# A two-layer graph attention kernel: which queue stores the packed mask, and the order of four partition quarters

## Chip, cores and metric

The kernel runs on one core of one Trainium2 chip. The metric is the device time of one execution in microseconds (us). Three executions of the kernel before took 2398.2, 2375.98 and 2375.66 us; the median is 2375.98 us.

## What is computed

`x` is 8192 nodes by 128 features (float32), `adj` an 8192 by 8192 matrix of int32 zeros and ones. Two layers follow each other; cut to what matters, each is:

```
h = maximum(layernorm(x), 0)
Wh = h @ W + b
e = leaky_relu((Wh @ a1)[:, None] + (Wh @ a2)[None, :], 0.2)
attention = softmax(where(adj > 0, e, -9e15), axis=1)
x = x + attention @ Wh
```

Both layers read the same 256 MB of adjacency. The result is `x` after the second layer.

## The kernel before, in words

The 8192 rows are cut into 64 tiles of 128 rows. Since leaky_relu of a sum has two slopes, exp of it splits into two products; a tile therefore needs only two 0/1 masks per edge (edge with positive sum, edge with negative sum), which `masks` holds as fp8 bytes. The rest is TensorE work: per tile 128 matmuls (line 546) of a mask chunk against `node_rows`, 64 chunks by 2 masks, into two PSUM banks.

**Stages.** (1) The node rows of layer 0 are made (about the first 195 us) and re-laid out by `load_rows` (line 276), whose transfers write 32 partitions each. (2) Layer 0, tiles 0 to 63. (3) A seam: the rows of layer 1 are loaded, mask bytes are fetched back. (4) Layer 1, tiles 0 to 63, which reads no adjacency any more.

**What layer 0 does for one tile.** SyncE (SP) loads the tile's adjacency, 4 MB of int32, in four row groups r of 32 rows. `adj_sb` has one 1 MB buffer per row group. A row group is four transfers of 256 KB: quarter a of the columns (2048 int32, 8 KB a row) goes to partitions 32a to 32a+31 (`load_adj`, line 250). Each row group's transfers wait for `cast_done`, that is until ScalarE has turned the same buffer of the tile before into bytes (`cast`, line 608: `sign_a<-adj_sb`). VectorE joins `sign_a` with the signs of the scores (`mask_bits`, line 824), transposes 32 by 32 blocks (`turn_bits`, line 845) and splits the two masks (lines 853 and 860). Then TensorE sums the tile. ScalarE (`part_one`, line 621) and VectorE (`finish_weigh`, line 869) take the PSUM banks over, and VectorE makes the new x.

**The mask bytes for layer 1.** Layer 0 also keeps the edge bits, two tiles in one byte tensor: VectorE's `pack` writes `pair_a` at an even tile (line 833) and adds the odd tile's bits (line 836), and raises `packed` each time. `pair_a` is one buffer of 1 MB. It is stored to `mask_dram` (line 325) by `store_pair`, a transfer of all 128 partitions, and the next even tile's `pack` (line 833) first waits for `pair_stored`. This happens 32 times, once a pair of tiles. Layer 1 reads the 32 MB back (`load_pair`, line 331) in place of `adj`.

**What sets the order.** Everything is written out by hand: each engine has its own program, the Tile helper gives the loop index, and `sweep` peels the first 4 and last 2 tiles around a loop of 2 tiles. All transfers of the kernel before are issued by SP, thus on one queue, in program order. In layer 0's loop SP issues, for tile T: the 16 transfers of adjacency of tile T+1, each group after its cast; on even T the store of pair T-1; then `store_x_new` of T-3 (line 263), `load_x_old` of T-1 (line 258), `store_rows` of T-4 (line 269). ScalarE's order for tile T is: `part_one` of T-1, then casts of T+2 mixed with `z_sign` (line 615) of T+2, `node_copy` (line 583) and `node_high` (line 594) of T-2. VectorE's order puts `pack` of T+1 between `mask_bits` and `turn_bits` of T+1, so a `pack` that waits holds the mask of that tile back too.

**The seam on SP.** After the last tile's loads SP issues the first four row reloads (line 276), two small stores, the last `store_pair`, waits until all pairs are stored, loads pair 0, and then issues the other reloads of `node_rows`.

Of the kernel before, what the change touches and what calls it, by code (L numbers as in the profile page):

```python
# [28 lines left out]
TILES = NODES // TILE  # L29
QUADS = 4  # L30
# [30 lines left out]
HEAD = 4  # L61
TAIL = 62
NODE_STEP = 4


class Tile:
# [36 lines left out]
def gat_kernel(nc, x, adj, w_0, b_w_0, a_vec_0, b_a_0, w_1, b_w_1, a_1, out):  # L103
# [3 lines left out]
    ds = bass.ds  # L107

    mask_dram = nc.dram_tensor("mask_bytes", (TILES // 2, 128, NODES), I8, kind="Internal").ap()
# [4 lines left out]
    with ExitStack() as ctx:  # L114
        def sb(name, shape, dt):
            return ctx.enter_context(nc.sbuf_tensor(name, shape, dt))
# [4 lines left out]
        def sem(name):  # L121
            return ctx.enter_context(nc.semaphore(name))
# [5 lines left out]
        pair_a = sb("pair_a", [128, NODES], I8)  # L128
# [71 lines left out]
        packed, pair_stored, pair_loaded = sem("packed"), sem("pair_stored"), sem("pair_loaded")  # L200
# [44 lines left out]
        @block.sync  # L245
        def _(sp):
            def load_adj(T, r):
                for a in range(QUADS):
                    sp.nop(nofuse=True)
                    sp.dma_start(adj_sb[QROWS * a:QROWS * (a + 1), r, :],  # L250
                                 adj[ds(T.t * TILE + QROWS * r, QROWS), SPAN * a:SPAN * (a + 1)]) \
                      .then_inc(adj_loaded[r], 16)
# [43 lines left out]
            def load_quadrant(a):  # L296
                for p in range(4):
                    sp.wait_ge(S[0].rows_stored[p], 16 * BLOCKS // 4 * (a + 1))
                for g in range(VGROUPS):
                    load_rows(0, a, g)  # L300

            adj_after = [BLOCKS, 2 * BLOCKS, 2 * BLOCKS + 3, 3 * BLOCKS]
            for a in range(QUADS):
                for k in range(BLOCKS * a, BLOCKS * a + NODE_STEP):
                    store_rows(0, Tile(k))
# [4 lines left out]
                if a:  # L310
                    load_quadrant(a - 1)
                with sp.Fori(BLOCKS // NODE_STEP * a + 1, BLOCKS // NODE_STEP * (a + 1)) as u:
                    for k in range(NODE_STEP):
                        store_rows(0, Tile(k, u, NODE_STEP))
            load_quadrant(QUADS - 1)
# [2 lines left out]
            load_x_old(0, Tile(0))  # L318
            load_x_old(0, Tile(1))

            def store_pair(T):

                sp.wait_ge(packed, T.t + 1)
                sp.nop(nofuse=True)
                sp.dma_start(mask_dram[ds(T.n, 1), :, :].rearrange("o p c -> p (o c)"), pair_a[:]).then_inc(pair_stored, 16)

            def load_pair(T):

                T.wait_before(sp, S[1].edge_bits, 1)
# [3 lines left out]
            def layer_0_tile(T):  # L333
                if T.plus(1).exists:
                    for r in range(RGROUPS):
                        sp.wait_ge(cast_done, RGROUPS * T.t + r + 1)
                        load_adj(T.plus(1), r)
                if T.p == 0 and T.plus(-1).exists:
                    store_pair(T.plus(-1))
                if T.plus(-3).exists:  # L340
                    store_x_new(0, T.plus(-3))
                    load_x_old(0, T.plus(-1))
                if T.plus(-4).exists:
                    store_rows(1, T.plus(-4))
# [14 lines left out]
            reload_rows(0)  # L359
            store_rows(1, Tile(TILES - 3))  # L360
            store_x_new(0, Tile(TILES - 2))
            store_pair(Tile(TILES - 1))
            sp.wait_ge(pair_stored, 16 * TILES // 2)
            load_pair(Tile(0))
            for g in range(1, VGROUPS - 1):
# [38 lines left out]
        def _(pool):  # L404
# [51 lines left out]
            for l in range(LAYERS):  # L456
# [14 lines left out]

                sweep(pool, body, trail=1 - l, step=[NODE_STEP, 2][l])


        @block.tensor
        def _(pe):
# [51 lines left out]

            sweep(pe, first_nodes, step=NODE_STEP)
            close_nodes(0)  # L530
# [48 lines left out]
        def _(act):  # L579
# [22 lines left out]
            def cast(T, r):  # L602

                if r == 0 and (T.u is not None or T.k >= 2):
# [3 lines left out]
                nc.scalar.activation(sign_a[:, T.p, SPAN * r:SPAN * (r + 1)], adj_sb[:, r, :], ACT.Sign, scale=-1.0) \  # L608
                  .then_inc(cast_done, 1)

            def z_sign(l, T, r):

                if r == 0:
                    T.wait_before(act, S[l].turned, 2)
                nc.scalar.activation(sign_z[:, T.p, SPAN * r:SPAN * (r + 1)], t_row[:], ACT.Sign, scale=-1.0,  # L615
                                     bias=neg_s[:, ds(RGROUPS * T.t + r, 1)]).then_inc(S[l].zsign_act, 1)

            def part_one(l, T):
                act.wait_ge(S[l].tile_summed, T.t + 1)
                T.wait_before(act, S[l].part_ac, 2)  # L620
                nc.scalar.activation(part_a[:, T.p, :], acc[T.p][0][:, 0:ROW], ACT.Copy, scale=coef_a[:, ds(T.t, 1)]) \  # L621
                  .then_inc(S[l].part_a, 1)
# [42 lines left out]
            def layer_0_tile(T):  # L665
                before, done, ahead = T.plus(-2), T.plus(-1), T.plus(2)
                if done.exists:
                    part_one(0, done)

                if ahead.exists:  # L670
                    cast(ahead, 0)
                if before.exists:
                    node_copy(1, before)
                if ahead.exists:
                    z_sign(0, ahead, 0)
                    cast(ahead, 1)
                    z_sign(0, ahead, 1)
                    cast(ahead, 2)
                if before.exists:
                    node_high(1, before)  # L680
                if ahead.exists:
                    cast(ahead, 3)
# [567 lines left out]
```

## Time and profile before

| | |
|---|---|
| median of three runs | 2375.98 us |
| span of the profiled execution | 2374.6 us |
| outside the span, if the profiled execution took the median | 1.4 us |
| TensorE / VectorE / ScalarE busy | 2026.7 / 1662.7 / 1126.4 us |
| bytes moved by DMA | 390.99 MB |
| mean granted TensorE clock, share of full | 0.938 |

The span is the time from the first to the last instruction on the core. A busy time counts what an engine executes, not what it waits for; a busy TensorE is not TensorE at its peak, since matmuls are pipelined. DMA share is the mean share of time in which the core's 16 DMA engines have a packet under way (1.02 reads as all of it), and GB/s is what they moved in that time: the two together tell whether packets are slow or absent.

### The profile page before, as it was taken

To read this page: it belongs to the slowest core of one execution; us is meant where nothing else is said; L and a number is where in the kernel's file an instruction comes from. 1 tells how busy PE (TensorE), PEld (TensorE's weight loads), DVE (VectorE), ACT (ScalarE), POOL (GpSimd) and SP (SyncE) were. 2 spreads that over 40 slices of the span, in tenths; PEclk is the share of its full clock that TensorE was granted. 3 is DMA by queue.
4 is the path that set the end of the run, shared out by engine and by line. 5 is a ranking of instruction groups with operands and counts; after the bars stand their busy time and mean duration, and the time that the engine had idled before them with its cause. 6 is when DMAs were issued, how large, how long until landed. Compare 5 with 4: busy or idle time off the path is not lost.

```text
span 2374.6 us, 49371 instructions
## 1 busy us (share of the span) xinstructions
PE 2026.7 (85%) x16866; PEld 1717.7 (72%) x16866; DVE 1662.7 (70%) x2685; ACT 1126.4 (47%) x1097; POOL 355.7 (15%) x496
## 2 busy tenths in 40 slices
PE   5545787887978788897888977999999999999998
PEld 3234676776867667676767765888888888888887
DVE  6662757786776868677687756777777777777774
ACT  4445566665766656675666613222333222233320
POOL 6530112222222212222222220000000000000000
PEclk9997898998989898998989988999999999999999
DMA  5669999999999999999999955111111111111110
GB/s 145 153 149 230 239 258 260 275 255 268 277 251 268 253 264 257 276 269 248 268 273 285 240 136 124 57 47 45 44 44 44 44 44 46 44 44 44 44 50 22
DMA packets 121682, 390.99 MB, mean 165 GB/s; under 512 B 25136, under 2 KB 74544, under 8 KB 80688
## 3 DMA queue, kind: packets, MB, share of 16 engines
q1 hardware_dynamic: 121648, 390.56, 63.1%
q8 instruction: 18, 0.29, 0.1%
q14 instruction: 16, 0.13, 0.0%
HBM read 331.62 MB, written 58.85 MB: 164 GB/s over the span
## 4 chain that ended last, share of the span: by engine, by line
PE 46%; DMA 25%; ACT 10%; issue 9%; DVE 5%; SPq 3%; DVEq 0%; ACTq 0%; POOL 0%; POOLq 0%
PE acc L546 45%; DMA mask_bytes<-pair_a 18%; ACT sign_a L608 6%; DMA node_rows<-row_parts 3%; DMA adj_sb<-in_adj_dram 3%; DVE masks L845 3%; SPq L250 2%; ACT sign_z L615 2%; ACT b_and_d L594 1%; DVE ext L790 1%; ACT part_a L621 1%; SPq L269 0%; ACT row_parts L596 0%; SPq L276 0%; DVE numer L888 0%
## 5 line engine op out<-in xcount | busy, mean ns | idle before, releaser
L546 PE MATMUL acc<-node_rows,masks 128*128 128x258 f16 x16384 | 1925.3, 279 | 255.8 <-ACT part_a L621 193.6
L546 PEld LDWEIGHTS acc<-node_rows,masks 128*128 128x128 fp8e4 x16384 | 1632.3, 100 | 526.5 <-issue 258.7
L608 ACT ACTIVATE sign_a<-adj_sb 128x2048 int8<-128x2048 int32 x256 | 486.4, 1900 | 43.2 <-DMA adj_sb<-in_adj_dram 43.0
L615 ACT ACTIVATE sign_z<-t_row,neg_s 128x2048 int8<-128x2048 f32 x256 | 504.2, 1995 | 1.0 <-DVE masks L845 1.0
L621 ACT ACTIVATE part_a<-acc,coef_a 128x258 f32<-128x258 f32 x128 | 60.4, 472 | 759.4 <-PE acc L546 759.4
L809 DVE TENSOR_SCALAR sign_z<-t_row,neg_s 128x2048 int8<-128x2048 f32 x256 | 326.7, 1278 | 7.4 <-issue 6.8
L845 DVE STREAM_TRANSPOSE masks<-sign_z 128x2048 uint32<-128x2048 uint32 x128 | 294.9, 2304 | 0.1
L869 DVE SCALAR_TENSOR_TENSOR part_ac<-acc,coef_c,part_a 128x258 f32<-128x258 f32 x128 | 62.0, 484 | 303.4 <-ACT part_a L621 303.4
L443 POOL TENSOR_TENSOR h_sum<-h_sum,ext 128x128 f32<-128x128 f32 x126 | 113.2, 899 | 895.6 <-DVE ext L790 892.0
L833 DVE TENSOR_SCALAR pair_a<-sign_a 128x2048 uint32<-128x2048 uint32 x32 | 39.2, 1227 | 290.9 <-DMA mask_bytes<-pair_a 290.9
L594 ACT ACTIVATE b_and_d<-ext 128x2 f32<-128x2 f32 x128 | 25.7, 201 | 321.8 <-DVE ext L790 273.7
L824 DVE SCALAR_TENSOR_TENSOR sign_z<-sign_z,sign_a 128x2048 uint32<-128x2048 uint32 x64 | 146.2, 2284 | 23.2 <-ACT sign_z L615 23.2
L853 DVE TENSOR_SCALAR masks<-masks 128x2048 uint32<-128x2048 uint32 x128 | 155.7, 1217 | 0.1
L860 DVE TENSOR_SCALAR masks<-masks 128x2048 uint32<-128x2048 uint32 x128 | 155.7, 1216 | 0.1
L431 POOL TENSOR_TENSOR rstd<-var_eps,minus_half 128x1 f32<-128x1 f32 x128 | 125.4, 981 | 152.0 <-DVE var_eps L726 151.7
L824 DVE SCALAR_TENSOR_TENSOR sign_z<-sign_z,pair_a 128x2048 uint32<-128x2048 uint32 x64 | 146.2, 2285 | 1.4 <-ACT sign_z L615 1.3
L498 PE MATMUL ps_h<-w_ext,centred_t 128*128 128x133 f32 x256 | 75.8, 389 | 49.5 <-ACT centred_t L583 46.0
L797 DVE SCALAR_TENSOR_TENSOR row_parts<-ext,b_and_d,row_parts 128x129 f16<-128x129 f32 x256 | 88.6, 347 | 36.9 <-ACT row_parts L596 36.6
L498 PEld LDWEIGHTS ps_h<-w_ext,centred_t 128*128 128x128 f32 x256 | 51.6, 251 | 66.4 <-ACT centred_t L583 56.0
L453 POOL TENSOR_SCALAR row_parts<-ext,b_and_d 128x129 f16<-128x129 f32 x64 | 84.1, 1313 | 0.0
L583 ACT COPY centred_t<-ps_t 128x128 f32<-128x128 f32 x128 | 32.3, 253 | 98.5 <-PE ps_t L493 98.4
L836 DVE SCALAR_TENSOR_TENSOR pair_a<-sign_a,pair_a 128x2048 uint32<-128x2048 uint32 x32 | 73.0, 2280 | 0.0
(81 smaller groups left out, 596.5 us busy)
## 6 DMA issues: line engine op xcount, KB each, us to landing
adj_sb<-in_adj_dram SPq DMA_DIRECT2D x1024, 256.0 KB, 9.8
mask_bytes<-pair_a SPq DMA_DIRECT2D x32, 1024.0 KB, 14.4
pair_a<-mask_bytes SPq DMA_DIRECT2D x32, 1024.0 KB, 4.8
node_rows<-row_parts SPq DMA_DIRECT2D x128, 129.0 KB, 7.6
node_rows<-node_rows SPq DMA_DIRECT2D x32, 516.0 KB, 11.5
x_old<-in_x_dram SPq DMA_DIRECT2D x64, 64.0 KB, 10.6
x_after_layer<-x_new SPq DMA_DIRECT2D x64, 64.0 KB, 10.3
x_old<-x_after_layer SPq DMA_DIRECT2D x64, 64.0 KB, 1.8
```

The source lines that it names most:

```text
L431: pool.tensor_tensor(rstd[:, T.p, :], var_eps[:, T.p, :], minus_half[:], ALU.pow).then_inc(S[l].rstd, 1)
L443: pool.tensor_tensor(h_sum[:], h_sum[:], ext[:, T.p, 0:DIM], ALU.add).then_inc(S[l].h_sum, 1)
L498: pe.matmul(ps_h[:, 0:EXT], centred_t[:, T.p, :], w_ext[l][:], start=True, stop=True).then_inc(S[l].h_raw, 1)
L546: mm = pe.matmul(acc[T.p][s][:, 0:ROW], stationary[s][:, c // BYTES, c % BYTES, :], node_rows[:, c, ROW * s:ROW * (s + 1)], start=(c == 0) ...
L608: nc.scalar.activation(sign_a[:, T.p, SPAN * r:SPAN * (r + 1)], adj_sb[:, r, :], ACT.Sign, scale=-1.0) \
L615: nc.scalar.activation(sign_z[:, T.p, SPAN * r:SPAN * (r + 1)], t_row[:], ACT.Sign, scale=-1.0, bias=neg_s[:, ds(RGROUPS * T.t + r, 1)]).t ...
L797: ins = nc.vector.scalar_tensor_tensor(out=row_parts[:, slot, ROW * s + PART:ROW * (s + 1)], in0=ext[:, T.p, 0:PART], scalar=b_and_d[:, T. ...
L809: nc.vector.tensor_scalar(sign_z[:, T.p, SPAN * r:SPAN * (r + 1)], t_row[:], neg_s[:, ds(RGROUPS * T.t + r, 1)], -1.0, ALU.is_gt, ALU.mult) \
L824: nc.vector.scalar_tensor_tensor(out=bits, in0=bits, scalar=LOW_Z_WORD[T.p], in1=edges, op0=ALU.bitwise_xor, op1=ALU.bitwise_and).then_inc ...
L845: nc.vector.transpose(g2[:, T.p, :].bitcast(U32).rearrange("p (b r i) -> p r b i", r=RGROUPS, i=QROWS), sign_z[:, T.p, :].bitcast(U32).rea ...
L853: nc.vector.tensor_scalar(g1[:, T.p, :].bitcast(U32), words, SHIFT_G1[T.p], EDGE_WORD, ALU.logical_shift_left, ALU.bitwise_and).then_inc(S ...
L860: nc.vector.tensor_scalar(words, words, SHIFT_G2[T.p], EDGE_WORD, ALU.logical_shift_left, ALU.bitwise_and).then_inc(S[l].g_ready, 1)
```

## The change

Two edits. First, `load_adj` issues the four quarters of a row group in the order 0, 2, 1, 3 in place of 0, 1, 2, 3; sizes, addresses and semaphores stay. Second, `store_pair` leaves SP's program and goes to ScalarE's: the same transfer, after the same wait on `packed`, is issued on ScalarE's own DMA queue in odd tiles T, right behind `part_one` of T-1. The stored pair is the one whose second tile is T. SP keeps its wait for `pair_stored` in the seam.

```
+QUAD_ORDER = (0, 2, 1, 3)
...
             def load_adj(T, r):
-                for a in range(QUADS):
+                for a in QUAD_ORDER:
...
-            def store_pair(T):
-
-                sp.wait_ge(packed, T.t + 1)
-                sp.nop(nofuse=True)
-                sp.dma_start(mask_dram[ds(T.n, 1), :, :].rearrange("o p c -> p (o c)"), pair_a[:]).then_inc(pair_stored, 16)
-
...
-                if T.p == 0 and T.plus(-1).exists:
-                    store_pair(T.plus(-1))
...
             store_x_new(0, Tile(TILES - 2))
-            store_pair(Tile(TILES - 1))
             sp.wait_ge(pair_stored, 16 * TILES // 2)
...
+            def store_pair(T):
+
+                act.wait_ge(packed, T.t + 1)
+                act.nop(nofuse=True)
+                act.dma_start(mask_dram[ds(T.n, 1), :, :].rearrange("o p c -> p (o c)"), pair_a[:]).then_inc(pair_stored, 16)
...
                 if done.exists:
                     part_one(0, done)
+                if T.p == 1 and T.exists and (T.u is not None or T.k < TILES):
+                    store_pair(T)
```

Place 1, SP in the loop of layer 0, the end of the even tile's adjacency loads. Before, the store stands between them and the small transfers:

```order
L250 DMA adj_sb<-in_adj_dram 32x2048
L325 ISA [waits packed]
L325 DMA mask_bytes<-pair_a 128x8192
L261 ISA
L263 ISA [waits fin_0]
L263 DMA x_after_layer<-x_new 128x128
L258 ISA [waits fin_0]
L258 DMA x_old<-in_x_dram 128x128
```

Of the change (its lines are numbered one or more higher):

```order
L251 DMA adj_sb<-in_adj_dram 32x2048
L262 ISA
L264 ISA [waits fin_0]
L264 DMA x_after_layer_0<-x_new 128x128
L259 ISA [waits fin_0]
L259 DMA x_old<-in_x_dram 128x128
```

The 1 MB store and its wait are gone from SP; what follows is issued in the same order.

Place 2, ScalarE in the loop of layer 0, the odd tile. Before:

```order
L621 ISA [waits part_ac_0,tile_summed_0]
L621 ACTIVATE part_a<-acc_0_0,coef_a 128x258
L607 ISA [waits packed,edge_bits_0]
L608 ACTIVATE sign_a<-adj_sb 128x2048 [waits adj_loaded_0]
L583 COPY centred_t<-ps_t_1 128x128 [waits h_raw_1,turned_ps_1]
```

Of the change:

```order
L619 ISA [waits part_ac_0,tile_summed_0]
L619 ACTIVATE part_a<-acc_0_0,coef_a 128x258
L607 REGISTER_ALU [waits packed]
L607 DMA mask_bytes<-pair_a 128x8192
L599 ISA [waits packed,edge_bits_0]
L600 ACTIVATE sign_a<-adj_sb 128x2048 [waits adj_loaded_0]
L575 COPY centred_t<-ps_t_1 128x128 [waits h_raw_1,turned_ps_1]
```

The store and its wait stand between the odd tile's `part_a` and its first cast. `tile_summed_0` is TensorE's end of a tile of layer 0.

Place 3, SP in the seam. Before, the last store, the wait for it and the reloads behind it:

```order
L269 DMA node_rows<-row_parts 128x516 [waits low_1]
L263 DMA x_after_layer<-x_new 128x128 [waits fin_0]
L325 DMA mask_bytes<-pair_a 128x8192 [waits packed]
L331 DMA pair_a<-mask_bytes 128x8192 [waits pair_stored]
L276 DMA node_rows<-node_rows 32x4x2064 [waits rows_free]
```

Of the change:

```order
L270 DMA node_rows<-row_parts 128x516 [waits low_1]
L264 DMA x_after_layer<-x_new 128x128 [waits fin_0]
L326 DMA pair_a<-mask_bytes 128x8192 [waits pair_stored]
L277 DMA node_rows<-node_rows 32x4x2064 [waits rows_free]
```

The wait for `pair_stored` stays at its place; the store that it waits for is now issued by ScalarE.

## Rows read from the trace of the kernel before

**Rows 1.** Profile page: DMA share in tenths and GB/s, 40 equal slices.
```profile
DMA  5669999999999999999999955111111111111110
GB/s 145 153 149 230 239 258 260 275 255 268 277 251 268 253 264 257 276 269 248 268 273 285 240 136 124 57 47 45 44 44 44 44 44 46 44 44 44 44 50 22
```
**Rows 2.** Profile page: the chain that ended last, by line.
```profile
PE acc L546 45%; DMA mask_bytes<-pair_a 18%; ACT sign_a L608 6%; DMA node_rows<-row_parts 3%; DMA adj_sb<-in_adj_dram 3%; DVE masks L845 3%; SPq L250 2%; ACT sign_z L615 2%; ACT b_and_d L594 1%; DVE ext L790 1%; ACT part_a L621 1%; SPq L269 0%; ACT row_parts L596 0%; SPq L276 0%; DVE numer L888 0%
```
**Rows 3.** Waits, whole span: total us, times, longest.
```profile
DVE pair_a L833 <- DMA mask_bytes<-pair_a: 290.9, 31, 14.6
...
ACT sign_a L608 <- DMA adj_sb<-in_adj_dram: 43.0, 22, 12.6
```
**Rows 4.** Chain in order of time: start, length; the 30 stores from first to last.
```profile
259.26 17.76 DMA mask_bytes<-pair_a
...
832.79 15.01 DMA mask_bytes<-pair_a
...
1357.45 16.13 DMA mask_bytes<-pair_a
```
**Rows 5.** Busy time of a stretch of layer 0; then PEclk, DMA share, GB/s.
```profile
300.00:1300.00 1000.00, 833.27 (x6950) 706.38 (x6948) 717.80 (x1102) 644.19 (x527) 220.42 (x209) 0.91 1.02 265
```
**Rows 6.** The same view, stretches of 2 us around one store.
```profile
839.00:841.00 2.00, 2.00 (x20) 1.75 (x18) 0.00 (x0) 2.00 (x2) 0.00 (x0) 1.00 1.05 246
...
843.00:845.00 2.00, 2.00 (x20) 1.75 (x19) 0.00 (x0) 0.09 (x1) 0.00 (x0) 1.00 0.97 381
...
857.00:859.00 2.00, 2.00 (x15) 1.58 (x14) 2.00 (x5) 0.26 (x2) 0.18 (x1) 0.74 1.01 234
```
**Rows 7.** The same view: row reloads onto one quarter; one pair load.
```profile
57.00:67.00 10.00, 3.52 (x9) 2.05 (x9) 4.43 (x21) 3.04 (x12) 3.59 (x9) 1.00 1.05 210
...
1514.00:1515.00 1.00, 1.00 (x11) 0.88 (x9) 1.00 (x3) 0.00 (x0) 0.00 (x0) 1.00 0.95 401
```
**Rows 8.** Timeline of SP: start, length, what it issues.
```profile
820.27 12.24 SPq L250 DMA_DIRECT2D adj_sb<-in_adj_dram  x16
832.79 0.37 SPq L325 DMA_DIRECT2D mask_bytes<-pair_a  x1
833.61 0.37 SPq L263 DMA_DIRECT2D x_after_layer<-x_new  x1
...
835.65 20.71 SPq L250 DMA_DIRECT2D adj_sb<-in_adj_dram  x16
```
**Rows 9.** Timeline of VectorE and ScalarE in the same stretch.
```profile
822.42 2.29 DVE L836 SCALAR_TENSOR_TENSOR pair_a<-sign_a,pair_a 128x2048 uint32<-128x2048 uint32 x1
...
833.15 0.48 ACT L621 ACTIVATE part_a<-acc,coef_a 128x258 f32<-128x258 f32 x1 [2.68 <-PE acc L546]
...
837.77 0.15 DVE L881 TENSOR_SCALAR empty<-joined 128x1 f32<-128x1 f32 x1
...
847.83 1.23 DVE L833 TENSOR_SCALAR pair_a<-sign_a 128x2048 uint32<-128x2048 uint32 x1 [9.91 <-DMA mask_bytes<-pair_a]
...
853.37 1.21 DVE L860 TENSOR_SCALAR masks<-masks 128x2048 uint32<-128x2048 uint32 x1
```
**Rows 10.** Profile page, DMA issues: count, KB each, median us to landing.
```profile
mask_bytes<-pair_a SPq DMA_DIRECT2D x32, 1024.0 KB, 14.4
pair_a<-mask_bytes SPq DMA_DIRECT2D x32, 1024.0 KB, 4.8
```
**Rows 11.** Seam: SP's own wait; then rows of the timeline.
```profile
SPq L330 <- DMA mask_bytes<-pair_a: 10.0, 1, 10.0
...
1416.74 5.53 SPq L276 DMA_DIRECT2D node_rows<-node_rows  x11
...
1456.21 4.05 PE L546 MATMUL acc<-node_rows,masks 128*128 128x258 f16 x18 [5.41 <-DMA node_rows<-node_rows]
```
**Rows 12.** TensorE: layer 1 in the chain; two groups of 300 to 1300 us.
```profile
1456.21 908.77 PE acc L546 x8096
...
L498 PE MATMUL ps_h<-w_ext,centred_t 128*128 128x133 f32 x106 | 20.6, 276 | 0.0
L493 PE MATMUL ps_t<-ident,centred 128*128 128x128 f32 x53 | 16.8, 317 | 0.0
```

## The prediction

> **What bounds the kernel now.** I read the page first. In its slices the DMA engines are full from slice 4 to slice 23 and nearly idle behind that [rows 1]: layer 0 streams the adjacency, layer 1 doesn't, so the change can act on the first 1400 us only. The chain that ended last names TensorE for 45% and then, before any other engine, the store of the packed pair, 18% [rows 2]. The waits say who suffers: VectorE stands 290.9 us, 31 times, before line 833 for that store, while ScalarE waits only 43.0 us for adjacency [rows 3]. Read alone, that makes latency of the store the bound.
>
> The chain in order of time gives the pace: from the store at 259.26 to that at 1357.45 us are 29 pairs, so 1098.19 / 29 = 37.9 us a pair of tiles [rows 4]. The stretch of 300 to 1300 us shows a DMA share of 1.02 at 265 GB/s [rows 5]. By the code a pair moves 32 x 256 KB of adjacency (8.39 MB), 1.05 MB of packed bytes, and 0.52 MB of x and node rows, in all 9.96 MB; 9.96 MB / 265 GB/s = 37.6 us. So the queue never runs dry, and the pace is the rate of the DMA engines. The store takes so long because it stands behind adjacency on the one queue. Removing VectorE's wait alone buys nothing as long as this rate stays: it would come back as ScalarE waiting for adjacency.
>
> The 2 us stretches show why the rate is low. With adjacency alone it is 234 to 246 GB/s at a full share; while the store's packets run it is 381, also at a full share [rows 6]. Busy engines that move less have slower packets. What differs is the destination: adjacency goes to 32 partitions a transfer, the store leaves all 128. Two more rows agree: row reloads onto one and the same quarter move 210 GB/s, and a pair load onto 128 partitions 401 [rows 7]. I take 210 for four transfers in a row into one quarter, 238 for the adjacency now, 385 for what is free of the quarter.
>
> The Trainium skill, page "SBUF — State Buffer", section "Door 1: The DMA port swizzle", says that partitions 0 to 31 reach 8 of the 16 SBUF ports and that 32 to 63 reach the same 8; the other two quarters share the other 8. By that rule, the order 0, 1, 2, 3 asks twice for one half, then twice for the other, and 0, 2, 1, 3 alternates. The trace agrees with the half rate [rows 6, 7]; which quarters share ports no row here shows.
>
> **Edit 1, the order.** Nothing is added or removed; 1024 transfers keep their size. Where the destination changes to another half, the tail of one transfer and the head of the next can run side by side. In time per MB (1.05 MB, one row group): at 210 GB/s 5.0 us with no change of half; at 238 4.4 us with two changes in a row group, so a change saves 0.3 us. With four changes it is 3.8 us, that is 276 GB/s. A pair has 8 row groups: 8 x (4.4 - 3.8) = 4.8 us saved. The bounds are 0 (238 stays) and 385 GB/s (2.7 us, saves 13.6, more than other bounds let through). Below nothing: 210, which is 5.0 us, 8 x 0.6 = 4.8 us lost. I take 276, since it goes by the two nearest rows; its weakness is that the 210 row has smaller packets.
>
> **Edit 2, the store on its own queue.** SP loses one issue, from 832.79 to 833.61, 0.8 us in two tiles [rows 8]; ScalarE gets it, and has room, 644 us busy in 1000 [rows 5]. When is it issued? `packed` is up at 822.42 + 2.29 = 824.7; ScalarE's `part_a` of the odd tile runs at 833.15 to 833.63 [rows 9]. So the store leaves at 833.6 in place of 832.8: no sooner, and ScalarE doesn't wait for `packed`. Behind it on ScalarE stand the cast, which waits for the same semaphore anyway, and so nothing is held. What changes is that it no longer stands behind up to 4 MB of adjacency. Landing now: median 14.4 us; a 1 MB transfer with empty queues: 4.8 us, of which 1.05 MB / 385 GB/s = 2.7 is moving [rows 10]. Interleaved one to one with adjacency the moving takes 5.4 to 7 us, so 7.5 to 9 us in all; bounds 4.8 and 14.4. VectorE reaches line 833 at 837.9 and the store lands about 842: the wait falls from 9.9 to some 4 us [rows 9].
>
> In bytes this edit moves nothing. It can help the rate a little, since a DMA engine that alternates a store packet and an adjacency packet leaves the quarter's share to others: at best 2.1 MB at 385 GB/s, 5.4 us, where now 4.4 + 2.7 = 7.1; between 0 and 1.7 us a pair. With edit 1 less is left; I take 0.3.
>
> **What is late next.** TensorE: layer 1 runs 8096 matmuls in 908.77 us, 0.112 each, so 14.4 a tile; layer 0 adds (20.6 + 16.8) / 53 = 0.7 [rows 12]: 15.1, or 30.2 us a pair. The path by the store: sent 0.5 us after a tile's end, landed after 7.5 to 9, then 853.37 + 1.21 - 847.83 = 6.75 us on VectorE until the next mask is ready [rows 9], in all 14.8 to 16.3 against 15.1: at most 1.2 us a pair more, 31.4. SP: 16 issues take 12.24 us, and 820.27 to 835.65 is 15.4 a tile with the store [rows 8]; without, 15.0 on the mean of a pair or less. All these lie under DMA.
>
> **Sum.** A pair by DMA: 37.9 - 4.8 - 0.3 = 32.8 us. Three other limits lie 1.4 to 2.6 us below, so some jitter will show; I add 0.2: 33.0. Saved: 4.9 us x 31 pairs = 152 us. The seam: SP waited 10.0 us for the last store, and 11 reloads went out only at 1416.74 [rows 11]. ScalarE now sends that store when TensorE's tile 62 ends, so the reloads go 6 to 10 us sooner; they end in TensorE's wait of 5.4 us, the most that can be saved [rows 11]. I take 5. In all 157 us. Against the span of 2374.6 us that gives 2217.6, and with the 1.4 us around it 2219 us; the median of the runs is 2375.98, and the same 157 off gives 2219 too.
>
> **The rivals.**
> - B, the queue is no longer the bound. If the alternation brings adjacency to 310 GB/s or more (27 us a pair), then TensorE with the path by the store sets the pace, 30.2 to 31.4 us. Taking 31.2: 6.7 x 31 = 208, and 5 for the seam: 2163 us. For it: the 381 GB/s in the same kernel [rows 6]. Against it: DMA engines take their packets in order, so halves overlap at the edges of transfers only.
> - C, the order changes little. DMA engines work through 8 KB packets one by one and all come to a quarter together; two edges more may give nothing. Then only the interleaving pays, some 1 us a pair, and the seam: 31 + 5 = 36, 2340 us. For it: the share is full and packets have no gaps that an order could fill. The Trainium skill, page "SBUF — State Buffer", section "“Can I just issue two DMAs to hit both halves?”", says that two transfers to the two halves gained 6% over one. By that rule adjacency would go at 252 GB/s, 2.0 us a pair less, and C would be at 2278. The rows of 210 and 238 GB/s differ by 13% for half the edges [rows 6, 7], more than that rule would let me expect.
> - D, slower. Neighbouring transfers to one half run at 238 now, not 210, because the DMA engines have drifted apart along the queue. If the mix of halves at each edge makes them wait for one another, adjacency falls to 210 GB/s: 4.8 us a pair, 149 us, less 5: 2520 us. It decides from the point where adjacency moves less than about 232 GB/s, when the loss eats the 1 us of interleaving. Against it: nothing in the rows shows mixed traffic slower than unmixed.
> - E, the change doesn't do what it says: the store's queue gets no turn until the other is empty, and the order is without effect. 2376 us less the seam, 2371.
>
> **How the numbers follow.** Forecast 0.55, own range 2190 to 2260 (286 to 250 GB/s for adjacency); B 0.20; C 0.17; D 0.03; E 0.05. To leave out no more than 0.2 the range takes in B down to 2150 and C's better part up to 2325. A measurement of this kernel can tell about 1% from no change, 24 us. Faster by over that are the forecast, B, and 0.14 of C: 0.89. Within it are E and the rest of C: 0.08. Slower: D, 0.03.
>
> **What would show it.** Right: 2 us stretches with adjacency alone at 265 to 290 GB/s and a full share; pairs 33 us apart; the store landing in 7 to 9 us; VectorE's wait at line 833 under 130 us in all; ScalarE's wait for adjacency above 43 us, since DMA still bounds; the granted clock nearer to 1, as TensorE's gaps shrink. Wrong: adjacency still at 238 GB/s (C); a DMA share clearly under 1 in layer 0 (B: the bound has moved); the store still landing in 14 us (E).

## The result and the profile after

The changed kernel takes 2263.46 us, the median of four runs (2258.86 to 2267.36). In the same comparison the kernel before took 2387.09 us (median of four, 2375.66 to 2433.69). The ratio is 0.952, interval [0.945, 0.959]: faster by 4.8%. The forecast was 2219 us; 44 us of the 157 us forecast as saved did not come. In all that follows, medians are of all runs of a kernel, and a ratio with an interval compares only the runs within 1.5% of the fastest of each kernel. The profiled execution has a span of 2264.2 us, 110.4 less than before.

Where the 110.4 us went can be read from TensorE's rows. Both kernels begin tile 0 at the same time (176.84 us before, 176.64 after). Its timeline at the seam, before:

```profile
1402.59 8.89 PE L546 MATMUL acc<-node_rows,masks 128*128 128x258 f16 x78
1438.26 12.54 PE L546 MATMUL acc<-node_rows,masks 128*128 128x258 f16 x96 [11.00 <-DVE masks L860]
```

and after (start, length, what):

```profile
1300.45 8.89 PE L538 MATMUL acc<-node_rows,masks 128*128 128x258 f16 x78
1336.33 8.85 PE L538 MATMUL acc<-node_rows,masks 128*128 128x258 f16 x62 [10.99 <-DVE masks L860]
```

Layer 1 after, as one piece of the chain:

```profile
1336.33 918.41 PE acc L538 x8192
```

Layer 0 ended at 1411.5 us and now at 1309.3: 102 us. From there to the first matmul of layer 1 it takes 27 us in both. Layer 1 took 926.7 us (1438.26 to 1456.21 + 908.77, [rows 12]) and takes 918.4: 8 us, of which 5.4 are TensorE's wait for the row reloads [rows 11], now gone. So 102 us are for the two edits in layer 0, and 8 for the seam and the start of layer 1.

The page after, slices, the chain by line and the store's issues:

```profile
DMA  5659999999999999999999681111111111111110
GB/s 145 161 141 243 254 292 280 288 294 309 309 304 269 282 277 278 286 273 288 282 285 296 180 189 47 46 46 46 46 46 46 46 46 46 46 46 46 45 45 11
...
PE acc L538 58%; DMA adj_sb<-in_adj_dram 12%; DMA mask_bytes<-pair_a 11%; DVE masks L845 2%; DMA node_rows<-row_parts 2%; ACT sign_a L600 2%; SPq L251 1%; DVE ext L790 1%; ACT part_a L619 1%; PE ps_h L490 0%; ACT b_and_d L586 0%; ACT row_parts L588 0%; DMA masks<-in_x_dram 0%; DVE row_parts L797 0%; SPq L277 0%
...
mask_bytes<-pair_a ACTq DMA_DIRECT2D x32, 1024.0 KB, 10.8
```

Against [rows 1] the slices 6 to 22 are as full, but carry 269 to 309 GB/s in place of 248 to 285. Against [rows 2] the store's share fell from 18% to 11% and adjacency rose from 3% to 12%. Against [rows 10] the store lands after 10.8 us in place of 14.4.

The waits after (total us, times, longest), against [rows 3]:

```profile
DVE pair_a L833 <- DMA mask_bytes<-pair_a: 179.8, 31, 7.6
...
ACT sign_a L600 <- DMA adj_sb<-in_adj_dram: 137.7, 98, 9.6
```

VectorE's wait fell by 111 us, ScalarE's wait for adjacency rose by 95. The chain in order of time shows the change of pace:

```profile
464.17 14.95 DMA adj_sb<-in_adj_dram
...
495.95 10.21 DMA mask_bytes<-pair_a
...
1260.92 10.38 DMA mask_bytes<-pair_a
```

From 495.95 to 1260.92 are 22 pairs, 34.8 us each, where [rows 4] gave 37.9. Up to 495.95 the chain goes from tile to tile through adjacency. From there to the end of layer 0 it holds no adjacency transfer at all; it goes round one loop a pair, of which this is one turn:

```profile
698.25 11.29 DMA mask_bytes<-pair_a
...
716.58 4.03 PE acc L538 x18
...
725.36 8.74 PE acc L538 x78
734.41 12.14 DMA mask_bytes<-pair_a
```

The store lands after 11.3 us. Within 7.0 us more VectorE has made the masks of the next even tile, ScalarE has freed a PSUM bank, and TensorE begins. It sums that tile in 17.5 us; then ScalarE takes the sum over (`part_one`) and issues the next store. The turn takes 36.2 us here, 34.8 on the mean. The tile takes 17.5 us and not the 14.7 of an unhindered one since the first 18 matmuls need 4.03 us, twice the usual time each: from 716 to 721 us, after a stop of 4 us, the granted clock is 0.50. So in most of layer 0 the changed kernel is held by the store's way round, not by the DMA rate. Busy times of four stretches (PE, PEld, DVE, ACT, POOL; then PEclk, DMA share, GB/s):

```profile
300.00:1200.00 900.00, 802.59 (x6771) 681.60 (x6769) 708.35 (x1089) 640.79 (x520) 213.22 (x208) 0.95 1.02 287
703.00:704.00 1.00, 1.00 (x11) 0.90 (x9) 0.00 (x0) 1.00 (x1) 0.00 (x0) 1.00 0.94 256
705.00:706.00 1.00, 1.00 (x11) 0.87 (x10) 0.00 (x0) 1.00 (x1) 0.00 (x0) 1.00 1.03 428
708.00:709.00 1.00, 1.00 (x11) 0.88 (x10) 0.00 (x0) 0.23 (x1) 0.00 (x0) 1.00 1.02 239
```

The first row is the one to compare with [rows 5]: the same full share, 287 GB/s for 265. The other three lie around one store, which the timeline shows from its issue to VectorE's use of the buffer:

```profile
698.25 0.34 ACTq L607 DMA_DIRECT2D mask_bytes<-pair_a  x1
...
709.57 1.23 DVE L833 TENSOR_SCALAR pair_a<-sign_a 128x2048 uint32<-128x2048 uint32 x1 [6.75 <-DMA mask_bytes<-pair_a]
```

The store is issued at 698.25 us. The rate stays at adjacency's level until 704, is 359 to 431 GB/s from 704 to 708, and falls back. The trace also counts packets by queue; q1 is SP's, q10 ScalarE's (packets, MB, share of 16 engines). From 698 to 703 us:

```profile
q1 hardware_dynamic: 225, 1.24, 100.3%
```

and from 704 to 707:

```profile
q10 hardware_dynamic: 125, 0.93, 73.7%
q1 hardware_dynamic: 268, 0.26, 25.0%
```

So the store's packets start some 5 us after the issue, although its own queue is empty (a median of 5.3 us over the 32 stores), and then they take most of the engines: 0.93 of the 1.19 MB moved in these 3 us are the store's, and adjacency all but stands still. In packets of 8 KB, from 300 to 1100 us, one of the store takes a median of 309 ns and one of SP's queue 505.

### The profile page after: what moved, and what is told of

It reads as the page before. It is cut to its first block, busy times and chain, and to the rows that moved or that the text cites. A ratio compares the mean times of both kernels' runs of the same rounds, so it can differ in the third digit from the quotient of the medians.

```text
span 2264.2 us, 49373 instructions
## 1 busy us (share of the span) xinstructions
PE 2015.0 (89%) x16866; PEld 1710.1 (76%) x16866; DVE 1664.7 (74%) x2685; ACT 1134.8 (50%) x1097; POOL 347.0 (15%) x496
## 4 chain that ended last, share of the span: by engine, by line
PE 59%; DMA 25%; DVE 5%; issue 4%; ACT 3%; SPq 2%; DVEq 0%; ACTq 0%; POOL 0%; POOLq 0%
PE acc L538 58%; DMA adj_sb<-in_adj_dram 12%; DMA mask_bytes<-pair_a 11%; DVE masks L845 2%; DMA node_rows<-row_parts 2%; ACT sign_a L600 2%; SPq L251 1%; DVE ext L790 1%; ACT part_a L619 1%; PE ps_h L490 0%; ACT b_and_d L586 0%; ACT row_parts L588 0%; DMA masks<-in_x_dram 0%; DVE row_parts L797 0%; SPq L277 0%
## 5 line engine op out<-in xcount | busy, mean ns | idle before, releaser
L600 ACT ACTIVATE sign_a<-adj_sb 128x2048 int8<-128x2048 int32 x256 | 487.4, 1904 | 142.3 <-DMA adj_sb<-in_adj_dram 137.7
L833 DVE TENSOR_SCALAR pair_a<-sign_a 128x2048 uint32<-128x2048 uint32 x32 | 39.3, 1227 | 179.8 <-DMA mask_bytes<-pair_a 179.8
L445 POOL TENSOR_SCALAR row_parts<-ext,b_and_d 128x129 f16<-128x129 f32 x64 | 75.3, 1176 | 17.3 <-ACT b_and_d L586 17.2
L485 PE MATMUL ps_t<-ident,centred 128*128 128x128 f32 x128 | 49.4, 388 | 19.6 <-DVE centred L723 18.4
## 6 DMA issues: line engine op xcount, KB each, us to landing
mask_bytes<-pair_a ACTq DMA_DIRECT2D x32, 1024.0 KB, 10.8
```

## The experiments

All ratios are to the kernel before, run in the same comparison on the same chip. The first question: which edit did it?

### The order alone, the queue alone

`e1_order_only` is the kernel before with the new order; `e2_queue_only` is the changed kernel with the old one.

```
 # e1: store_pair back in SP's program, at its old place
+                for a in (0, 2, 1, 3):
 # e2
-QUAD_ORDER = (0, 2, 1, 3)
+QUAD_ORDER = (0, 1, 2, 3)
```

> The kernel before with the order 0, 2, 1, 3 alone; the store stays on SP's queue. Theory 1 (the pace is the DMA rate, and the order raises the rate of adjacency): adjacency alone moves about 250 GB/s in 2 us stretches as in the changed kernel, and the time is some 2300 to 2330 us, about half of the way or more; the store still lands in 14 us. Rival (the store's latency sets the pace): the rate doesn't matter, the store stands as long behind adjacency, and the time stays within 1% of before, 2360 us or more.

> The changed kernel with the old order 0, 1, 2, 3; the store goes by ScalarE's queue. Theory 1: adjacency alone stays at 238 GB/s, the store lands in 10 to 11 us, and since bytes and rate stay the time falls only by the seam and some interleaving: 2330 to 2365 us. Rival (latency sets the pace): the store lands 4 us sooner, 31 times, so that 2376 falls to 2250 to 2270, the whole gain, without any help of the order.

Measured: e1 2292.82 us, ratio 0.966 [0.958, 0.974]; e2 2282.5 us, 0.954 [0.942, 0.967]. Each edit gains by itself: 3.4% and 4.6%. The two together gain 4.8%, so the gains overlap almost wholly. The stretch of 300 to 1100 us, e1:

```profile
300.00:1100.00 800.00, 710.68 (x6003) 605.37 (x6002) 625.65 (x964) 558.45 (x459) 194.38 (x184) 0.94 1.02 286
```

e2:

```profile
300.00:1100.00 800.00, 719.72 (x6095) 612.18 (x6093) 635.22 (x975) 577.64 (x466) 192.07 (x187) 0.95 1.02 291
```

and the changed kernel:

```profile
300.00:1100.00 800.00, 712.88 (x6028) 605.71 (x6026) 628.04 (x967) 568.76 (x461) 187.91 (x184) 0.95 1.02 288
```

The kernel before has 263 GB/s there. All three sit at one level, whichever edit brought them to it. (The profiled e2 is its fastest run, 2258.99 us.) In e1 VectorE still waits 210.2 us for the store, in e2 167.6. The queue edit alone, which I had priced at 0.3 us a pair, raised the rate by 28 GB/s. What the two have in common is the store's landing, e1 first:

```profile
mask_bytes<-pair_a SPq DMA_DIRECT2D x32, 1024.0 KB, 11.2
mask_bytes<-pair_a ACTq DMA_DIRECT2D x32, 1024.0 KB, 11.0
```

Against 14.4 us before [rows 10] the order alone saves 3.2 us on it, where I had expected 14 still, the queue alone 3.4, both 3.6. Times 31 that is 99, 105 and 112 us; the profiled spans fell by 93.5, 117.4 and 110.4. By these numbers the gains don't add because each edit shortens the same landing, to nearly the same length.

### Orders with the same, or fewer, changes of half

Call quarters 0 and 1 one half, 2 and 3 the other. Then 0, 1, 2, 3 changes half twice in a row group (the step from 3 to the next 0 counted), and 0, 2, 1, 3 four times. `e3_order_0231` has another order with two changes; `e4_one_change` alternates two orders, with one. Both keep the store on ScalarE's queue.

```
 # e3
+QUAD_ORDER = (0, 2, 3, 1)
 # e4
-                for a in QUAD_ORDER:
+                for a in ((0, 1, 2, 3), (2, 3, 0, 1))[r % 2]:
```

> The changed kernel with the order 0, 2, 3, 1: again two changes between the lower and the upper 64 partitions in a row group, as in 0, 1, 2, 3 (0 to 2 and 3 to 1, with none from 1 to the next 0). Theory 1 (changes of half count): adjacency alone at 238 GB/s, time as e2. Rival (any other order than ascending, or adjacent quarters, matter: here no quarter follows its upper neighbour but for 2, 3): about 250 GB/s and 2264 us, as the changed kernel.

> The changed kernel with 0, 1, 2, 3 for even row groups and 2, 3, 0, 1 for odd ones: one change of half in a row group, half as many as before. Theory 1: a change saves 0.2 us of a row group's 4.4 (4 changes 248 GB/s, 2 changes 238), so one change gives about 4.5 to 4.7 us, 225 to 233 GB/s, and the kernel is slower than e2 by 8 x 0.15 x 31 = 40 to 70 us: 2380 to 2430 us. Rival (DMA engines have drifted apart, the order has no say; something else gave the gain): same as e2.

Measured: e3 2304.05 us, 0.968 [0.958, 0.979]; e4 2371.17 us, 0.999 [0.987, 1.011]. Against e2, in the same comparison, e4 is 4.6% slower (0.999 against 0.954), and the intervals don't touch: the order matters, in the direction of the count of changes. e3 has e2's count and e2's interval overlaps with its own. e4 at 350 to 400 us:

```profile
350.00:400.00 50.00, 39.83 (x336) 33.46 (x333) 35.71 (x58) 29.58 (x26) 9.50 (x12) 0.97 1.03 252
```

What adjacency itself does is seen in stretches of 1 us. Of the 50 from 450 to 500 us the median is 238 GB/s in e4, 243 before, 266 in the changed kernel, but 262 in e3 and 353 in e2, which like the kernel before change half twice: one such stretch doesn't sort the orders. The slow end of all 900 from 300 to 1200 us does. A quarter of them move at most 221 GB/s with one change (e4); 229 to 245 with two (before, e2, e3 and, below, e6 and e10); 254 to 265 with four (the changed kernel, e1 and, below, e5, e8 and e13). So the order sets a low level. Over 300 to 1100 us e4 moves 267 GB/s and e2 291; beside the lower level, e4 seldom runs faster than it, which the experiments below come to. From 500 to 1200 us the chains of e3 and e4 go through adjacency alone and hold no store: their landing is 10.9 us as in the changed kernel, but there the rate is the limit.

### Without the wait for the store

If the rate is what the DMA engines give, as I had argued, then taking VectorE's wait away gains nothing. `e5_no_wait` (from the changed kernel) and `e6_before_no_wait` (from the kernel before) store the same number of bytes from `node_rows`, so that nothing has to wait for the store. Layer 1 then does the same work on other edge bits, and the result is another.

```
-   act.dma_start(mask_dram[...], pair_a[:]).then_inc(pair_stored, 16)
+   act.dma_start(mask_dram[...], node_rows[...].bitcast(I8)[:, 49536:49536 + NODES]).then_inc(pair_stored, 16)
...
-                    if T.u is not None or T.k:
-                        dve.wait_ge(pair_stored, 16 * T.n)
 # e6: the same two edits with sp in place of act, in the kernel before
```

> The changed kernel with VectorE's wait for the pair store taken away: the 1 MB store reads from a part of node_rows that nothing writes in layer 0, and pack no longer waits for it; the bytes moved stay. The edge bits for layer 1 are then not the right ones; layer 1 does the same work on them. Theory 1 (the rate of the full DMA queue sets the pace): VectorE's wait of 180 us turns up again as ScalarE's wait for adjacency, and the time stays within 1% of the changed kernel, 2240 to 2285 us. Rival 1 (the store's path sets the pace now): a pair falls from 34.8 us to 31, 2150 to 2170 us. In between, 2190 to 2230, would mean that the rate itself rises when the engines press harder.

> The same edit made to the kernel before (order 0, 1, 2, 3, store on SP's queue, read from node_rows, no wait in pack; layer 1 again gets other edge bits). Theory 1, as the prediction said: removing VectorE's wait of 291 us alone buys nothing, 2340 to 2390 us. Rival (the wait is the loss): 31 x 6.5 us less, some 2180 us.

Measured: e6 2266.99 us, 0.951 [0.941, 0.962]; e5 2189.29 us (2126.11 to 2201.21), a quotient of the medians of 0.918 (2383.6 before), without an interval. The wait did cost time: 4.9% by e6, with one queue, the old order and the same number of bytes. My step is refuted, though a good part of it holds: in e6 the wait does come back at ScalarE, where [rows 3] had 43.0 us,

```profile
ACT sign_a L609 <- DMA adj_sb<-in_adj_dram: 323.4, 162, 10.3
```

and of VectorE's 291 us only 117 are gained. From 500 to 1200 us the chain of the kernel before holds no adjacency transfer, and ScalarE waits 1.5 us for adjacency; in e6 adjacency is 63% of the chain, and ScalarE waits 177 us. So before, the store's way round was the limit, and only without the wait is the DMA rate. The windows of e6 at 350 and at 900 us, to be read against the 265 GB/s at a share of 1.02 of [rows 5] and the 246 GB/s of [rows 6]:

```profile
350.00:400.00 50.00, 38.85 (x318) 32.40 (x315) 34.34 (x54) 27.87 (x25) 8.52 (x10) 0.89 1.03 259
...
900.00:950.00 50.00, 45.62 (x400) 39.30 (x401) 42.93 (x66) 39.59 (x33) 10.16 (x12) 1.00 1.01 302
```

Here is what a DMA share hides: both rows are full, one moves 259 GB/s and the other 302. A full share says that a packet is always under way on each engine, not how long each takes. At 246 GB/s and full share, 16 engines take 16 x 8192 B / 246 GB/s = 533 ns for a packet of one row's 8 KB; at 350 GB/s they take 374 ns. The trace's own packets agree: the median 8 KB packet takes 536 ns in the kernel before and 489 in e6. What I took for a fixed rate is elastic.

### Half of the adjacency's bytes

`e7_half_bytes` loads only half the columns of each quarter from the second tile on; its result is another.

```
+                    n = SPAN if T.u is None and T.k == 0 else SPAN // 2
+                    sp.dma_start(adj_sb[QROWS * a:QROWS * (a + 1), r, 0:n], ...
```

> The changed kernel with half of the adjacency bytes: from tile 1 on each transfer brings only the first 1024 of its 2048 columns, the rest of the buffer keeps tile 0's values, so the result is another. It measures what is left when DMA has ample room. Both theories: DMA share near 0.6, adjacency never waited for. The forecast's next bound is TensorE with the path by the store: 30.2 to 31.4 us a pair, 2130 to 2165 us; the store lands in under 6 us. If the pair stays at 33 or more, a chain of engines that I haven't seen bounds the kernel next.

Measured: 2077.63 us, 0.870 [0.863, 0.877]. Its stretch:

```profile
300.00:1100.00 800.00, 800.00 (x7155) 700.86 (x7153) 747.09 (x1144) 661.41 (x542) 226.60 (x217) 1.00 0.64 193
```

and two pieces of its chain in order of time:

```profile
995.19 10.74 PE acc L539 x96
...
1009.85 10.74 PE acc L539 x96
```

TensorE is busy throughout at the full clock, and its tiles stand 14.66 us apart, 29.3 us a pair. This is the next bound (forecast: 30.2), and the DMA share here is well under 1. Nothing else on VectorE, ScalarE or SP stands in the way of that pace. The store lands in 4.6 us, and VectorE waits for it 2.5 us in all.

### The store one tile earlier

`pair_a` is complete long before ScalarE reaches `part_one`. `e8_store_early` issues it after the third cast of the even tile, one tile earlier in ScalarE's program.

```
-                if T.p == 1 and T.exists and (T.u is not None or T.k < TILES):
-                    store_pair(T)
...
+                if T.p == 0 and T.plus(1).exists:
+                    store_pair(T.plus(1))
```

> The changed kernel with the store of a pair issued one tile earlier in ScalarE's order, behind the third cast of the even tile, when packed has just come, some 5 us sooner than now. The result is the same as before. Theory 1 (rate of the full queue): VectorE's wait shrinks, ScalarE's wait for adjacency grows, time within 1% of the changed kernel, 2240 to 2285 us. Rival (the store's path sets the pace): 3 to 4 us a pair less, 2140 to 2180 us.

Measured: 2234.92 us, 0.936 [0.924, 0.948]; its four runs were 2204.22, 2221.9, 2247.94 and 2267.47. It does the whole computation. The issue no longer waits for TensorE's end of a tile, which opens the loop shown above, and VectorE's wait is gone:

```profile
DVE pair_a L833 <- DMA mask_bytes<-pair_a: 4.4, 9, 1.6
```

Two stretches of e8, both without that wait:

```profile
350.00:400.00 50.00, 50.00 (x449) 43.81 (x448) 46.46 (x72) 43.62 (x34) 11.62 (x12) 1.00 1.02 356
...
650.00:700.00 50.00, 44.13 (x368) 37.30 (x366) 39.48 (x62) 35.41 (x29) 9.00 (x12) 0.93 1.03 285
```

In the first the DMA engines give 356 GB/s, TensorE is busy in all 50 us at full clock, and its tiles are 14.65 us apart, as in e7. In the second, 300 us later in the same execution of the same loop, they give 285 and TensorE has gaps again. The medians of the 1 us stretches are 336 GB/s (400 to 450 us) and 261 (650 to 700). So one program, in one execution, runs at very different rates with the engines full. From 500 to 1200 us its chain is 78% adjacency: here the rate is the limit.

### The early store with the old order, and a repeat

`e10_early_0123` is e8 with `QUAD_ORDER = (0, 1, 2, 3)`. `e13_store_early_again` is e8 unchanged.

> e8 (store one tile earlier on ScalarE's queue) with the old order 0, 1, 2, 3. With the wait gone, what is the order worth? Theory 1 (adjacency in step moves about 246 GB/s with two changes of half and 258 with four, and in the stretches where DMA engines are out of step both orders run at 300 or more): 1 to 2 us a pair dearer, 2255 to 2290 us against e8's 2235. Rival (the order is worth nothing once VectorE doesn't wait, as e2 against the changed kernel hints): within 0.5% of e8.

> e8 once more, with more rounds, to be set beside e10 (same kernel with the old order: ratio 0.9088, single times 2149 to 2370 us) and beside the changed kernel (0.9519). If the order is worth something once the wait is gone: ratio below 0.90. If it is worth nothing: 0.90 to 0.95, overlapping e10. In either case below 0.945 makes the earlier store better than the changed kernel. If DMA engines fall in and out of step by chance within a run, the single times spread by 2% or more, as in e8 and e10, against 0.4% for the changed kernel.

Measured: e10 2244.29 us, seven runs between 2149.46 and 2369.98, in a comparison whose kernel before took 2421.01. The ratio of 0.909 [0.895, 0.922] rests on the two fastest of the seven; the medians give 0.927. e13 2205.18 us (six runs, 2171.25 to 2258.81), against 2383.11 in its comparison 0.925, without an interval. e10 at 450 and at 900 us:

```profile
450.00:500.00 50.00, 50.00 (x449) 43.81 (x448) 47.62 (x73) 42.67 (x36) 13.86 (x13) 1.00 1.02 337
...
900.00:950.00 50.00, 41.33 (x352) 35.02 (x349) 34.29 (x54) 31.27 (x26) 8.20 (x10) 0.97 1.03 255
```

The medians of the 1 us stretches are 352 and 242 GB/s. The low level is that of the kernel before (243), the high one as high as e8's. So the order does not set the high level. It may be that the share of the time at it decides an execution, which fits that e10's runs differ by 10%; only one of them was profiled. With the order 0, 2, 1, 3 the runs of e8 and e13 lie between 2171 and 2267. Which order is better for the early store stays open: the two were not run in one comparison.

### Adjacency on two queues

`e11_two_queues` is e8 with quarters 0 and 1 issued by SP and 2 and 3 by ScalarE; `e12_one_quarter` gives only quarter 3 to ScalarE.

```
+SP_QUADS = (0, 1)      # e12: (0, 2, 1)
+ACT_QUADS = (2, 3)     # e12: (3,)
...
+            def load_share(T, r):
+                if T.exists:
+                    act.wait_ge(cast_done, RGROUPS * T.plus(-1).t + r + 1)
+                    for a in ACT_QUADS:
+                        act.nop(nofuse=True)
+                        act.dma_start(...).then_inc(adj_loaded[r], 16)
```

> e8 with the four transfers of a row group on two queues from tile 1 on: SP issues quarters 0 and 1, ScalarE quarters 2 and 3, each after the same cast. Theory (a DMA engine takes packets from the two queues in turn, so it changes half with every 8 KB packet, and two DMA engines that share a port are rarely both on it): adjacency alone at 285 GB/s or more, pairs near the 29.3 us that e8 reached in its best stretches: 2130 to 2190 us. Rival (the DMA engines finish what was queued first, as the store's 5.4 us from issue to first packet suggests, or ScalarE's 8 more issues a tile hold its own work up): 2220 to 2300 us.

> As e11, with only quarter 3 on ScalarE's queue and 0, 2, 1 on SP's: half of ScalarE's added issues, and one packet in four from the other queue. Theory: between e8 and e11, 2170 to 2220 us. Rival (ScalarE's added issues are what costs in e11): better than e11.

Measured: e11 2315.15 us, 0.963 [0.951, 0.975]; e12 2287.82 us, 0.954 [0.945, 0.963], both with the kernel before at 2421.01 us. Neither median beats e10's 2244.29 from the same comparison. e11 at 450 and at 900 us:

```profile
450.00:500.00 50.00, 38.16 (x314) 32.17 (x313) 37.55 (x52) 30.88 (x26) 8.02 (x9) 0.89 1.03 266
...
900.00:950.00 50.00, 43.06 (x345) 36.16 (x346) 36.20 (x58) 35.78 (x29) 10.18 (x12) 0.88 1.02 274
```

The medians of the 1 us stretches are 262 GB/s in both. If the engines took packets from the two queues in turn, this would be the strongest form of alternation tried; no run here shows whether they do. Its median is at the level of the order 0, 2, 1, 3, its slow end not: a quarter of the stretches move at most 241 GB/s. VectorE waits only 45.1 us in all for its store, so this low rate is not its stall's doing.

## Why the prediction was right and wrong

**The direction and the seam were right.** Layer 0 alone changed in pace, with the seam's 5.4 us beside it (forecast 5). The share stayed at 1.02, the clock rose from 0.938 to 0.963, ScalarE's wait for adjacency rose above 43 us, and the last bound is TensorE, at 29.3 us a pair in e7. But ScalarE's wait, which I had named as the sign that DMA still bounds, says so for the first part of layer 0 only: from 500 to 1260 us it is 29 of the 137.7 us, and there the chain goes by the store.

**The step that failed first: "Removing VectorE's wait alone buys nothing as long as this rate stays."** The condition was the error, and before it the sentence "the pace is the rate of the DMA engines". If adjacency had been too slow, ScalarE would have waited for it; it waits 43.0 us in all [rows 3], 1.5 from 500 to 1200 us, while the chain named the store. The 37.9 us a pair were the store's way round, and the 265 GB/s their outcome. e6 took the wait away, changing only the tensor that the store reads, and the rate rose from 263 to 286 GB/s between 300 and 1100 us; 4.9% were gained. e2, which only shortened the wait (290.9 to 167.6 us), gained 4.6%. Edit 2 was priced at 0.3 us a pair and is worth about what the whole change is. I had read a share of 1.02 at 265 GB/s as the engines' rate, though the 381 GB/s of [rows 6] at a share of 0.97 showed that a full engine can be a slow one. Nor is the destination of 32 partitions a transfer what makes it slow, as I had read from [rows 6, 7]: the same transfers pass at 356 GB/s in e8. The Trainium skill, page "DMA: Bandwidth & Descriptors", section "Issuing engines are not separate DMA queues", says that issuing from several engines saves only the time of issue. By that rule e2 could gain at most SP's 0.8 us a pair [rows 8], 25 us in all or 1%; it gained 4.6%, since the store's landing fell from 14.4 to 11.0 us; that is where the trace and the rule part.

**Edit 1 was too large in size, and paid in another way.** I forecast 276 GB/s for adjacency, by 0.3 us for each change of half. Measured by medians of 1 us, from 450 to 500 us: 243 before, 266 in the changed kernel. In time per 1.05 MB that is 4.3 us for two changes and 3.9 for four, where I had 4.4 and 3.8. By the slow quarter of the stretches one change has 4.7 us, two 4.3 to 4.6, four 4.0 to 4.1, so a change is worth 0.1 to 0.5 us; whether the steps are equal this doesn't tell. In the kernel before, though, the rate was not the limit, so the term did not come as I had priced it: what e1 gained came by the shorter landing. By itself the order gives 3.4% (e1), and one change in place of two costs 4.6% when the store has its own queue (e4 against e2). On top of edit 2 it shows no gain beyond the noise: 0.952 [0.945, 0.959] against 0.954 [0.942, 0.967], from two comparisons. The sum of my two terms was 5.1 us a pair, 4.8 and 0.3; measured are 37.9 - 34.8 = 3.1 in the chain, or 102 us / 31 = 3.3 over layer 0. A first term too large and a second too small, for two edits that act on one landing: that the total came within 2% of the measured time is partly luck.

**The store's landing.** "Interleaved one to one" gave 7.5 to 9 us. It lands in 10.8: for 5 us none of its packets move, and then they run nearly alone, not one to one with adjacency's. VectorE's wait is therefore 179.8 us and not under 130. With no adjacency around it the store needs 3.9 us (the last one), so it is not the issue itself that takes 5 us; it appears that each DMA engine first works off what it has already fetched of the other queue. That reading fits but was not isolated.

**The rivals.** B named TensorE with the path by the store, 30.2 to 31.4 us a pair. TensorE's bound is real and is reached: e8 runs at 29.3 us a pair from 350 to 550 us, where the medians of 1 us are 307 to 355 GB/s, about the threshold of 310 that I had worked out. And the path by the store is what holds the changed kernel for most of layer 0, without the condition that I had set for it and at 34.8 us: the landing takes 10.8 us for my 7.5 to 9, and TensorE's tile up to 17.5 for my 15.1. I had put this path under DMA. (My sum puts three limits 1.4 to 2.6 us below 32.8; SP's, 30.0 us, is 2.8 below, and nothing hangs on it.) C (2340 us) fell with e4 against e2, though its statement that the order on its own adds little to the queue edit is what came out, for another reason. D and E fell: nothing is slower, and the store gets its turn. The range 2150 to 2325 holds the result; my own narrower one, 2190 to 2260, misses it by 3 us.

**What can't be said yet.** Most stretches lie at a low level that the order sets, and others reach 300 to 360 GB/s, with either order. Values between are as common (the medians by 50 us in e8 are 254 to 355), so two sharp levels are not shown. In the profiled kernel before these medians stay at 229 to 270 GB/s from 300 to 1200 us; in e2, e5, e6, e8, e10 and e13 they go above 320 and fall back. A picture that fits is that the 16 DMA engines fall in step, so that all ask for the same half at once, and that stores and gaps set them apart. No run here isolates that, and the amount of adjacency outstanding doesn't sort the kernels by rate (a transfer lands after a median of 9.6 us at 263 GB/s before, 7.4 at 286 in e1, 12.4 at 278 in e10, 9.7 at 309 in e8). Why packets take longer while the store's way round holds the kernel, so that the engines look full, stays open, and so does why the order shortens the store's landing. Two buffers for `pair_a` were not tried.

**The better version.** e8 and e13 are one kernel. Its ratio to the kernel before is 0.936 [0.924, 0.948], against 0.952 [0.945, 0.959] of the changed one, so the intervals overlap a little; the repeat took 2205 us, and nine of the ten runs are below the fastest of the changed kernel's four (2258.86). It costs nothing but the place of one issue.

## What to carry to other kernels

A full DMA share is not a rate limit by itself. See whether the engine that uses the stream waits for it, and what the chain in order of time goes through. Compare GB/s between stretches at the same full share: if they differ, a wait elsewhere may well be worth removing, and one run without that wait tells more than an argument from the totals. When two edits act on the same resource or the same wait, don't add their gains; run each alone. A transfer that frees a buffer should be issued as soon as its data are ready, however full the queues are, since its packets may start only microseconds later.

## What the runs showed of the hardware

- At a DMA share of 1.02 the same loop, bytes and packet sizes moved 244 GB/s (e6, 300 to 350 us) to 367 (e10, 400 to 450). Within one execution of e8 it was 356 and then 285 GB/s over 50 us. A packet of 8 KB took a median of 309 ns for the store on its own queue and 505 on SP's in the changed kernel.
- A stream of transfers to 32 partitions each has a slow end that goes by the order: a quarter of the 1 us stretches from 300 to 1200 us move at most 221 GB/s with one change of half in a row group, 229 to 245 with two and 254 to 265 with four (one, five and five kernels). The Trainium skill, page "SBUF — State Buffer", section "“Can I just issue two DMAs to hit both halves?”", says that two transfers to the two halves gain 6% over one and serialize. The step from the kernel before to the changed one is larger (254 / 229 is 11%), and the 356 GB/s over 50 us don't agree at all: of all bytes there only the store's tenth goes in transfers of 1 MB from all partitions.
- A store on a queue of its own, issued while the other queue was full, moved nothing for a median of 5.3 us and then all of its 1 MB in 4.6 us, with most of the engines to itself (0.93 of 1.19 MB from 704 to 707 us). The last store, with adjacency finished, sent its first packet after 0.9 us.
- Executions of one kernel on one core differed by 10% (e10: 2149.46 to 2369.98 us), while the changed kernel's four differed by 0.4%, e7's by 0.1%, and eleven of the kernel before by 4.7% (2313.64 to 2422.25 us).
